# Norms of a decoder: Sqrt on ScalarE and reciprocal on VectorE become one power of minus one half on GpSimd

## The reference

```python
def _layernorm(x, axis=-1, eps=1e-05):
    m = jnp.mean(x, axis=axis, keepdims=True)
    v = jnp.var(x, axis=axis, keepdims=True)
    return (x - m) / jnp.sqrt(v + eps)
...
    x = x + _L0_attn_ref(_layernorm(x, axis=-1), L0_attn_q_w, ...)
    x = x + _L0_xattn_ref(_layernorm(x, axis=-1), ctx_1024, ...)
    ...
    x = x + _L3_ffn_ref(_layernorm(x, axis=-1), L3_ffn_in_proj_w, ...)
    return x
```

## Time and profile before

| what | value |
|---|---|
| median of 3 runs | 2486.11 us (2483.11 to 2487.94) |
| the profiled execution | 2487.08 us |
| its span, first to last instruction | 2485.0 us |
| TensorE matmuls busy | 1851.5 us, 75% |
| VectorE busy | 1760.5 us, 71% |
| ScalarE busy | 1120.0 us, 45% |
| GpSimd busy | 707.7 us, 28% |

### The profile page before, as it was taken

How to read it: one execution, slowest core, us unless ns; L and a number is a source line. 1 busy time by engine, 2 the same in 40 slices (tenths; PEclk the granted TensorE clock), 3 DMA queues, 4 the chain that set the end, 5 groups by cost and what they waited for, 6 DMA issues and landing times. The chain is left out here.

```text
span 2485.0 us, 36889 instructions
## 1 busy us (share of the span) xinstructions
PE 1851.5 (75%) x11751; PEld 1096.4 (44%) x11763; DVE 1760.5 (71%) x5601; ACT 1120.0 (45%) x3109; POOL 707.7 (28%) x617
## 2 busy tenths in 40 slices
PE   6996889962887999979887875666555555556778
PEld 2654446441354766644454543333333333333343
DVE  4336352268775666657745778999999999997665
ACT  3653442251315777731232554555555555554411
POOL 1200044005433333310032421344333333331130
PEclk7998899976998999989997897666665665667979
DMA  5000000310000000000100000000000000000000
GB/s 214 2 1 1 29 26 27 104 65 1 2 2 1 2 2 1 0 1 0 72 24 1 1 1 1 1 1 1 1 1 1 1 1 1 1 1 1 1 0 18
DMA packets 10591, 37.76 MB, mean 15 GB/s; under 512 B 1344, under 2 KB 7488, under 8 KB 9136
## 3 DMA queue, kind: packets, MB, share of 16 engines
q1 hardware_dynamic: 8880, 33.04, 3.4%
q0 software_dynamic: 1536, 2.59, 0.4%
HBM read 30.15 MB, written 5.51 MB: 14 GB/s over the span
## 5 line engine op out<-in xcount | busy, mean ns | idle before, releaser
L3733 PE MATMUL psum<-work 32*128 32x256 f32 x512 | 130.3, 653 | 288.2 <-ACT work L3851 288.2
L3913 DVE MATCH_REPLACE8 work<-work 128x256 f32<-128x256 f32 x768 | 322.1, 497 | 0.0
L3976 POOL TENSOR_TENSOR work<-work 128x1024 f32<-128x1024 f32 x63 | 148.3, 2355 | 484.2 <-ACT work L3851 484.2
L3910 DVE MAX8 work<-work 128x8 f32<-128x256 f32 x768 | 283.0, 495 | 0.0
L3733 PEld LDWEIGHTS psum<-work 32*128 32x128 f32 x512 | 77.8, 310 | 314.4 <-ACT work L3851 159.1
L718 POOL TENSOR_TENSOR work<-work 128x256 f32<-128x256 f32 (+2 forms) x144 | 133.5, 946 | 226.2 <-DVE work L1006 226.2
L934 ACT ACTIVATE work<-work 128x128 f32<-128x128 f32 (+1 forms) x320 | 145.3, 457 | 19.9 <-DVE work L981 18.2
L3851 ACT ACTIVATE work<-work 128x256 f32<-128x256 f32 x256 | 129.0, 504 | 0.0
L3913 DVE MATCH_VALUE_LOAD work<-work 128x8 f32 x768 | 128.0, 167 | 0.0
L3758 PE MATMUL psum<-work,tiles 128*8 128x256 f32 x512 | 116.9, 609 | 8.2 <-ACT work L3861 7.4
L3978 POOL TENSOR_TENSOR work<-work 128x1024 f32<-128x1024 f32 x63 | 119.3, 1894 | 6.0 <-DVE work L3935 1.2
(11 more groups left out here) (621 smaller groups left out, 4647.3 us busy)
## 6 DMA issues: line engine op xcount, KB each, us to landing
big_weights<-L0f_dram SPq DMA_DIRECT2D x1, 6117.5 KB, 28.5
big_weights<-L_dram SPq DMA_DIRECT2D x1, 5772.0 KB, 17.1
big_weights<-L_dram SPq DMA_DIRECT2D x1, 4952.5 KB, 16.1
choice_rows<-tiles SPq DMA_DIRECT2D x2, 1024.0 KB, 10.2
tiles<-choice_rows SPq DMA_DIRECT2D x8, 256.0 KB, 4.9
big_weights<-L_dram SPq DMA_DIRECT2D x1, 2027.0 KB, 21.2
big_weights<-L_dram SPq DMA_DIRECT2D x1, 1630.5 KB, 13.2
big_weights<-L0f_dram SPq DMA_DIRECT2D x1, 1630.5 KB, 6.2
```

Source lines behind the costliest of these rows:

```text
L3733: mm = nc.tensor.matmul(scores(n)[:, u, :], qb[head, tile % 2, u % 2 * P:(u % 2 + 1) * P], kb[head, tile % 2, :], start=True, stop=True, t ...
L3910: ch.step(v.max(top8[:, n % 2, u, r, :], src[:, u, :]))
L3913: ins = v.match_replace(raw[:, n % 2, u, :], top8[:, n % 2, u, r, :], src[:, u, :], REPLACED)
L3976: ch.link(g.tensor_tensor(mine, mine, rest[:, n % 2], ALU.subtract))
```

## The change

The Sqrt on ScalarE becomes a scaled and biased copy (Identity) of the mean squares to `std`. GpSimd then raises that tile to the power minus one half, by a tensor_tensor with a column of -0.5 that is read again and again; the result goes to `inv` as before. VectorE's reciprocals are gone, and so is the warming Sqrt. For the second norm of the first block, TensorE now waits for the scalings that free its banks, since VectorE's own order no longer stands for that. The rest of the lines moves up by 6 to 10.

```diff
-    sq, std, inv, warm = a.take(N), a.take(2, Q), a.take(2, Q), a.take(1)
+    sq, std, inv = a.take(N), a.take(2, Q), a.take(2, Q)
...
                 for n in range(4 * pair, 4 * pair + 4):
+                    pe.wait_ge(c.normed.sem, c.normed.at(free_after[spread[n]]))
...
-            def invert(pair):
-                dve.wait_ge(c.rooted.sem, c.rooted.at(pair + 1))
-                nc.vector.reciprocal(inv[:, pair, :], std[:, pair, :]).then_inc(c.inverted.sem, 1)
...
-            invert(0)
-            scale(0)
-            scale(1)
-            invert(1)
-            for n in range(2, 2 * NC):
+            for n in range(2 * NC):
                 scale(n)
             if also is not None:
-                for pair in range(2):
-                    dve.wait_ge(c.rooted.sem, c.rooted.at(pair + 3))
-                    nc.vector.reciprocal(inv2[:, pair, :], std2[:, pair, :]).then_inc(c.inverted.sem, 1)
...
-            nc.scalar.activation(warm, c.w("one"), ACT.Sqrt)
-
...
-                nc.scalar.activation(std[:, pair, :], c.psum[:, stats[pair], 0:Q], ACT.Sqrt, bias=c.w(eps), scale=grow) \
+                nc.scalar.activation(std[:, pair, :], c.psum[:, stats[pair], 0:Q], ACT.Identity, bias=c.w(eps), scale=grow) \
...
         def _(pool):
+            for pair in range(2):
+                pool.wait_ge(c.rooted.sem, c.rooted.at(pair + 1))
+                nc.gpsimd.tensor_tensor(inv[:, pair, :], std[:, pair, :], c.w("minus_half").broadcast_to([P, Q]), ALU.pow).then_inc(c.inverted.sem, 1)
+            for pair in range(2 if also is not None else 0):
+                pool.wait_ge(c.rooted.sem, c.rooted.at(pair + 3))
+                nc.gpsimd.tensor_tensor(inv2[:, pair, :], std2[:, pair, :], c.w("minus_half").broadcast_to([P, Q]), ALU.pow).then_inc(c.inverted.sem, 1)
             if "gpsimd" in beside:
```

More of the change, by code:

```diff
@@ L459, in _ @@
                 for pair in range(2):
-                    nc.scalar.activation(std2[:, pair, :], c.psum[:, stats[pair], 0:Q], ACT.Sqrt, bias=c.w(also[1])) \
+                    nc.scalar.activation(std2[:, pair, :], c.psum[:, stats[pair], 0:Q], ACT.Identity, bias=c.w(also[1])) \
                         .then_inc(c.rooted.sem, 1)
@@ L4482, in lay_out @@
     L.add(sm, "one", np.ones((P, 1), np.float32))
-    for name, eps in (("eps5", 1e-5), ("eps6", 1e-6), ("eps12", 1e-12), ("eps56", 1e-11), ("minus_magic", -MAGIC), ("eps55", 1e-10), ("epsf", float(np.finfo(np.float32).eps))):
+    for name, eps in (("eps5", 1e-5), ("eps6", 1e-6), ("eps12", 1e-12), ("eps56", 1e-11), ("minus_magic", -MAGIC), ("minus_half", -0.5), ("eps55", 1e-10), ("epsf", float(np.finfo(np.float32).eps))):
         L.add(sm, name, np.full((P, 1), eps, np.float32))
```

## The result

The changed kernel takes 3278.07 us (median of 4 runs, 3277.18 to 3279.46), the kernel before 2487.03 on the same chip: 1.3176 times the time, 95% interval 1.3155 to 1.3197. That is slower by 791 us, outside the predicted range. The profiled execution has a span of 3277.4 us and a mean granted clock of 0.740, where before it was 2485.0 and 0.818.

What follows compares the result with a forecast made beforehand. No engine fills the span; each norm is a chain of four engines taking turns, twice, uncovered. 86.4 + 1.5 - 3.1 + 5.6 + 0.7 + 23.4 + 16.8 = +131.3; 2487.1 + 131.3 - 1.0 = 2617 us, range 2468 to 2760.

Steps and rivals of the forecast that it cites:

- X: Time of one GpSimd power over a 128x128 tile, taken as 3.3 us, with ends 0.46 and 6.6.
- the high bound: Upper end for one power on GpSimd: 60 operations run one by one, 6.6 us.
- the waits: TensorE's wait before the spreads, twice in each of 18 norms: 2.4 us more, 36 times, +86.4 us.
- the first norm's second pair: In the first norm two more powers stand behind the second on GpSimd, delaying the second scalings: +1.5 us.
- The norm that multiplies first: Norm without centring: its power need not wait for VectorE's four products or a table load, -3.1 us.
- GpSimd's order: The all-reduce trial moves behind both powers, +3.9 us; the next norm changes the library back, +1.7: together +5.6.
- Table loads: 18 fewer, hidden in centred norms; two later blocks gain some 0.3 each, the experts' new load costs 1.28: +0.7 us.
- 18 loads less: Rival: all 18 dropped table loads were on the path, 18 x 1.28 = 23 us gained, 2451 us; chance 0.03.
- TensorE's clock: Longer waits lower TensorE's granted clock: +23.4 us in 16 centred norms, +16.8 in the matmuls behind norms.
- The plain pass: Rival: a GpSimd power costs only a plain pass, 0.46 us, making the kernel 12.6 us faster, 2474 us; chance 0.19.
- The long dependent chain: Rival: a GpSimd power is a long chain of dependent steps, 6.6 us, +256.7, 2743 us; chance 0.21.

Runs made afterwards that it cites:

- the plain pass: The changed kernel with GpSimd's two powers in each norm replaced by multiplications of constants, same waits and signals: 2479.23 us, 0.9965 of the kernel before.
- the run with one power: The changed kernel with each norm's second pair of factors by VectorE's reciprocal, without a root, instead of GpSimd's power: 2914.93 us, ratio 1.1709.
- the list: The kernel before with ten chained GpSimd passes in a block at the start; 128 power columns take 20.78 us, one 0.55, a multiplication 452 ns.

## Why the prediction was wrong

**The step that failed** is the price of one power, X. It was put as "at least two functions of that sort", 3.3 us, from VectorE's division and from 60 operations, "a number I choose", with the same 60 one by one as the high bound, 6.6. Measured: 20.73 us, 6.3 times the value taken and 3.1 times the bound. Of a column's 159 ns the one way explains 2 x 5.5 x 2.12 = 23 and the bound 50. The error was to let a chosen number of operations close the range upwards: no row of before showed a function on GpSimd, so nothing there spoke against 20 us.

**The rest of the sum stood, partly by luck.** With 20.73 in the prediction's own formulas the waits are 36 x 19.83 = 713.9 us and the first norm's second pair is 2 x 20.73 - 5.15 = 36.3; with the other terms as predicted, -3.1 + 5.6 + 0.7 + 23.4 + 16.8, it comes to 2487.1 + 793.6 - 1.0 = 3279.7, where 3278.07 was measured. The waits and the clock in the norms are borne out one by one. That the whole meets within 2 us is partly luck: single stretches between norms moved by -2.6 to +6.7 us that no term foresaw, and the term for the table loads was too small. Term by term:

- *First norm.* It is 77.2 us longer, 36.1 more than an ordinary one; by the formula 36.3.
- *The norm that multiplies first.* Its first copy comes 1.81 us sooner after the norm in front. From there it is 37.9 us longer; its clock was low already, so the two waits alone would make 39.7, and the wait for the products that is gone makes up the 1.7: together -3.5, predicted -3.1.
- *GpSimd's order.* The stretch behind the trial is 4.4 us longer (predicted 3.9), the next norm 3.2 longer than its neighbours (predicted 1.7). That the order itself was to blame held only in part: the plain pass shows the same two losses, but turning the order back costs 22 us more. That the trial waits for the second power is shown by the run with one power: there it ends inside the norm, and the stretch behind is 0.6 us longer instead of 4.4.
- *Table loads.* The load new in the experts costs 1.29 us at once, as predicted, but the whole run with the loads dropped is 7.4 us above the kernel before, where the term was 0.7: what the new load sets off behind it was left out, and some 4 us are not explained. That 18 loads less were worth nothing bears out that they were hidden. The Trainium skill ("ScalarE: Activation LUTs", What ACT_TABLE_LOAD costs) gives about 1283 ns for the load and about 1380 ns for a drain with it. The row's 1.28 us agrees with the first; the drain does not show, since the activation behind the new load starts 0.02 us after its end.
- *TensorE's clock.* Predicted 23.4 in the norms and 16.8 behind them; keeping TensorE busy gave back 23.2 and 20.2 in the profiles, 41 us by the medians. That the clock was the cause in the norms is shown by that run, by durations and granted clock; the 20.2 is a sum of stretches of which each moves by some us from run to run.

**The rivals.** The plain pass was priced at 2474 us, 12.6 below the kernel before, and ran in 2479, by the ratio 8.7 below: that branch was worked out rightly to some 4 us and did not happen. The long dependent chain had the right direction, at 2743 us. The runs bear out that the power is priced by the column and not by partition or value. Whether a column's 159 ns are a chain of dependent steps, no run shows. The Trainium skill's rule of 4 cycles for an element of such a chain ("GPSIMD Engine Reference", section 7) stays untested here.

**Open.** Between the sixth and the seventh norm the changed kernel is 6.7 us longer and the plain pass 7.0, without a power in it; 2.8 of that stood in a kernel with no edit there. The windows over the same matmuls show where it lies, first two pieces of the kernel before, then the same two of the plain pass:

```profile
614.87:634.36 19.49, 15.64 (x228) 7.02 (x220) 14.38 (x31) 8.47 (x23) 6.50 (x14) 0.91 0.01 2
701.59:716.44 14.85, 13.50 (x225) 10.11 (x226) 10.01 (x12) 1.82 (x4) 2.08 (x3) 1.00 0.01 2
```

```profile
610.47:633.75 23.28, 20.72 (x228) 9.72 (x228) 14.65 (x31) 8.87 (x24) 6.50 (x14) 0.63 0.01 1
701.47:718.74 17.27, 15.92 (x224) 11.72 (x226) 10.01 (x12) 1.82 (x4) 2.08 (x3) 0.80 0.01 2
```

TensorE's busy time is longer at a lower granted clock, by 3.8 and 2.4 us of the stretch, while the other engines work as long as before. In the changed kernel the second piece takes 17.38 us at 0.81, and a piece ahead of both 41.40 at 0.66 where before it took 36.77 at 0.72. Why the clock falls in these places in one run and not in another stays open.

## What to carry to other kernels

An operation that no row shows on its engine has no upper bound in the rows of other engines: measure one instruction before placing 36 of them on a chain, or leave the range open upwards. Where a chain has nothing beside it, the sum is count times price, and the price deserves the work; here everything but the powers and the waits for them came to some 40 us of 791. By the prediction's sum a power on GpSimd breaks even at 0.81 us, which by the list is (0.81 - 0.39) / 0.159, some 3 columns; by the plain pass, 8.7 us faster with 0.40 us a step, it is 0.40 + 8.7 / 36 = 0.64 us, not 2 columns. Both are estimates, as no run had so narrow a power.

## What the runs showed of the hardware

- GpSimd's power takes 159 ns a column and 0.39 us fixed, on 16 partitions as on 128, for both exponents tried (-0.5 and 1) and for a base of ones.
- GpSimd's library changes cost both ways: 5.6 to 5.9 us of "issue" in front of an all-reduce behind other work, 6.64 in front of a multiplication behind an all-reduce.
- Behind 15.6 us of matmuls and an idle of 4.81 us, averages took 1.10 us instead of 0.66; with waits of 0.52 and 1.17 the granted clock stayed at 1.00.
- The same matmuls between two norms took 19.49 us at a granted clock of 0.91 in one run and 23.28 at 0.63 in another, with no edit there.
- The first spreads of 64 columns took 0.18 us each, of 128 columns 0.15, both after a long wait: halving the width saved nothing and doubled the count.
